# Attention rows: GpSimd adds the attended values to x, and the row's work stands in another order around the transposed maxima

## What is computed

```python
def _L0_xattn_ref(q, k, v):                      # q = x (16,128,256), k = v = ctx_512 (16,128,64)
    QH, KVH = (32, 8)
    D = E // QH                                  # 8
    G = QH // KVH                                # 4
    qh = q.reshape(b, s, KVH, G, D).transpose(0, 2, 3, 1, 4)
    kh = k.reshape(b, s, KVH, D).transpose(0, 2, 1, 3)
    vh = v.reshape(b, s, KVH, D).transpose(0, 2, 1, 3)
    scores = jnp.einsum('bkgsd,bktd->bkgst', qh, kh) * scale
    attn = jax.nn.softmax(scores, axis=-1) / DROPOUT
    out = jnp.einsum('bkgst,bktd->bkgsd', attn, vh)
    return out.transpose(0, 3, 1, 2, 4).reshape(b, s, E)
...
x = _layernorm(x + _L0_xattn_ref(x, ctx_512, ctx_512), axis=-1)
```

## Time and profile before

| | us |
|---|---|
| three runs: median (lowest to highest) | 863.64 (862.07 to 865.16) |
| the profiled execution, its own time | 863.73 |
| its span, first to last instruction | 861.9 |
| TensorE busy, share of the span | 758.5, 88% |
| VectorE busy | 636.6, 74% |
| ScalarE busy | 437.3, 51% |
| GpSimd busy | 345.8, 40% |

### The profile page before, as it was taken

One profiled execution on the slowest core, in us unless ns is written; L12 is line 12 of the kernel. 1 busy time (PEld: TensorE's weight loads), 2 busy tenths in 40 slices (PEclk: granted clock), 3 DMA queues, 4 the chain that ended last, 5 costly groups with the idle time before them and its releaser, 6 DMA issues. The chain is left out here.

```text
span 861.9 us, 18011 instructions
## 1 busy us (share of the span) xinstructions
PE 758.5 (88%) x5790; PEld 403.6 (47%) x5795; DVE 636.6 (74%) x1094; ACT 437.3 (51%) x790; POOL 345.8 (40%) x349
## 2 busy tenths in 40 slices
PE   4699999999999999999999999954689999695773
PEld 1355555555555555555555555533233333243342
DVE  5578677678686687686686887867777778648995
ACT  6444445744455744444754444424367777542333
POOL 5573443754243835333753543316020000105572
PEclk8799999999999999999999999975799999998997
DMA  6721111331211151111112112011140000014411
GB/s 212 309 83 70 76 49 49 113 143 49 96 50 49 50 205 49 49 73 73 49 49 97 49 49 94 4 25 33 24 179 19 19 13 20 6 52 163 179 49 49
DMA packets 23332, 66.13 MB, mean 77 GB/s; under 512 B 7024, under 2 KB 11632, under 8 KB 17648
## 3 DMA queue, kind: packets, MB, share of 16 engines
q1 hardware_dynamic: 23312, 65.90, 20.9%
HBM read 62.55 MB, written 2.42 MB: 75 GB/s over the span
## 5 line engine op out<-in xcount | busy, mean ns | idle before, releaser
L241 POOL TENSOR_TENSOR cum_rows<-cum_rows,cum_t 128x512 f32<-128x512 f32 x128 | 135.8, 1071 | 203.8 <-DMA cum_rows<-cum_scratch 203.8
L560 PE MATMUL pring<-xt_hi,w_hi 128*128 x576 | 172.9, 382 | 6.1 <-DVE gate L485 4.5
L560 PE MATMUL pring<-xt_lo,w_hi 128*128 x576 | 172.3, 381 | 0.0
L560 PE MATMUL pring<-xt_hi,w_lo 128*128 x576 | 171.9, 380 | 0.0
L461 DVE TENSOR_TENSOR bt<-pring,bt 128x512 f16<-128x512 f32 x128 | 88.0, 687 | 73.6 <-ACT bt L333 73.5
L333 ACT CAST bt<-pring 128x512 f16<-128x512 f32 x128 | 74.5, 582 | 129.1 <-PE pring L560 128.9
L465 DVE TENSOR_TENSOR ct<-pring,ct 128x512 f16<-128x512 f32 x128 | 87.9, 687 | 52.9 <-ACT ct L337 52.6
L572 PEld LDWEIGHTS pscore<-ct,bt 128*128 128x128 f16 x1548 | 96.1, 98 | 34.9 <-issue 8.9
L572 PE MATMUL pscore<-ct,bt 128*128 128x128 f16 x1548 | 107.6, 219 | 1.7 <-issue 0.8
L813 DVE TENSOR_REDUCE mx<-bank_at 128x4 f32<-128x512 f32 x128 | 83.1, 677 | 28.3 <-PE bank_at L904 28.0
L337 ACT CAST ct<-pring 128x512 f16<-128x512 f32 x128 | 74.7, 583 | 54.4 <-PE pring L560 54.4
(11 more groups left out here) (153 smaller groups left out, 945.9 us busy)
## 6 DMA issues: line engine op xcount, KB each, us to landing
cum_rows<-cum_scratch SPq DMA_DIRECT2D x32, 1024.0 KB, 4.6
w_raw<-in_w_in SPq DMA_DIRECT2D x36, 256.0 KB, 5.4
weight_b<-weight_scratch SPq DMA_DIRECT2D x8, 1024.0 KB, 6.7
mt<-in_xt SPq DMA_DIRECT2D x4, 512.0 KB, 6.8
acc<-in_x SPq DMA_DIRECT2D x1, 2048.0 KB, 12.0
vals<-in_vals SPq DMA_DIRECT2D x16, 128.0 KB, 2.0
out<-acc SPq DMA_DIRECT2D x4, 512.0 KB, 2.9
w_raw_e<-in_w_up SPq DMA_DIRECT2D x1, 1024.0 KB, 5.0
```

What stands on the lines that cost most here:

```text
L241: nc.gpsimd.tensor_tensor(rows[:, par, q], rows[:, par, q], own, ALU.subtract).then_inc(sem("since"), 1)
L560: mm = nc.tensor.matmul(bank[name][:], w[:, c, k, cols], x[:, k, bass.ds(n % TB, 1), :].rearrange("p o n -> p (o n)"), start=(i == 0), sto ...
```

## The change

It has four parts.

1. `add_heads` moves from VectorE to GpSimd. VectorE's last two adds at the end go too. Where VectorE's own adds ordered its uses of `att`, `divide` now waits until GpSimd has done the add of two divisions earlier (`x_add`); the count starts at one. On GpSimd the adds of rows 0 and 1 stand ahead of the three weight casts, those of rows 2 to 12 in a loop behind them, and the last six between the inverse roots.
2. VectorE's plan: `/0'` goes ahead of M0, and `s1'` stands between M2 and M3, `/1'` between M4 and M5.
3. ScalarE's row: N goes ahead of e1, and `evac_out` of the row before goes behind e2.
4. TensorE's plan: X0 goes from behind F0 D0 to behind F0 D0 F1 F2, D1 D2 follow A1' together, F3 F4 F5 stand together ahead of T1', D3 D4 behind it.

```diff
         @block.gpsimd
         def _(pool):
+            pool.sem_inc(sem("x_add"), 1)
...
+            def add_heads(b, t):
+                pool.wait_ge(sem("att"), 2 * b + t + 2)
+                x = acc[:, bass.ds(b, 1), t * P:t * P + P]
+                nc.gpsimd.tensor_tensor(x, x, att[:, t].unsqueeze(1), ALU.add).then_inc(sem("x_add"), 1)
...
+            for b in range(2):
+                for t in range(2):
+                    add_heads(b, t)
             for i, (name, w) in enumerate((("w_up", w_up), ("w_gate", w_gate), ("w_down", w_down))):
                 pool.wait_ge(sem(f"in_{name}"), 16)
                 nc.gpsimd.tensor_copy(w[:], w_raw[:, i]).then_inc(sem("w_bf16"), 1)
             pool.wait_ge(sem("w_bf16"), 3)
 
+            with pool.Fori(2, BATCH - 3) as b:
+                for t in range(2):
+                    add_heads(b, t)
             pool.wait_ge(sem("in_small"), 16 * 5)
-            for t in range(TB - 1):
-
-                pool.wait_ge(sem("ln_var"), t + 1)
-                r = rstd[:, t * NB:t * NB + NB]
-                nc.gpsimd.tensor_tensor(r, r, expo[:, 0:NB], ALU.pow).then_inc(sem("ln_rstd"), 1)
+            add_heads(BATCH - 3, 0)
+            inverse_root(0)
+            add_heads(BATCH - 3, 1)
+            inverse_root(1)
+            add_heads(BATCH - 2, 0)
+            inverse_root(2)
+            add_heads(BATCH - 2, 1)
+            add_heads(BATCH - 1, 0)
+            add_heads(BATCH - 1, 1)
...
                 exponential(b, 0)
-                exponential(b, 1)
                 if not last:
                     negate_max(b + 1, 1 - slot)
+                exponential(b, 1)
+                exponential(b, 2)
                 if not first:
                     evac_out(b - 1, 1)
-                for i in range(2, 6):
+                for i in range(3, 6):
                     exponential(b, i)
...
             def divide(b, t):
                 dve.wait_ge(sem("rsum"), 2 * b + t + 1)
+                dve.wait_ge(sem("x_add"), 2 * b + t)
...
-            plan = "M0 /0' M1 +0' M2 M3 s1' M4 /1' M5 +1' M6 M7 s0".split()
+            plan = "/0' M0 M1 M2 s1' M3 M4 /1' M5 M6 M7 s0".split()
...
-            plan = "F0 D0 X0 F1 A1' D1 F2 D2 F3 T1' D3 F4 D4 F5 A0 D5 F6 D6 F7 T0 D7".split()
+            plan = "F0 D0 F1 F2 X0 A1' D1 D2 F3 F4 F5 T1' D3 D4 A0 D5 F6 D6 F7 T0 D7".split()
```

More of the change, by code:

```diff
@@ L724, in _, with inverse_root @@
             nc.gpsimd.tensor_tensor(ctx_parts[:, 1, BATCH:], ctx_t[:, BATCH:], ctx_parts[:, 0, BATCH:], ALU.subtract).then_inc(sem("ctx_lo"), 1)
+            def add_heads(b, t):
+                pool.wait_ge(sem("att"), 2 * b + t + 2)
+                x = acc[:, bass.ds(b, 1), t * P:t * P + P]
+                nc.gpsimd.tensor_tensor(x, x, att[:, t].unsqueeze(1), ALU.add).then_inc(sem("x_add"), 1)
+            def inverse_root(t):
+                pool.wait_ge(sem("ln_var"), t + 1)
+                r = rstd[:, t * NB:t * NB + NB]
+                nc.gpsimd.tensor_tensor(r, r, expo[:, 0:NB], ALU.pow).then_inc(sem("ln_rstd"), 1)
+            for b in range(2):
+                for t in range(2):
+                    add_heads(b, t)
             for i, (name, w) in enumerate((("w_up", w_up), ("w_gate", w_gate), ("w_down", w_down))):
@@ L843, in divide @@
                 dve.wait_ge(sem("rsum"), 2 * b + t + 1)
+                dve.wait_ge(sem("x_add"), 2 * b + t)
                 nc.vector.tensor_tensor(att[:, t].rearrange("p (g k d) -> p g k d", k=4, g=4), pturn4[:, :, :, 0:8],
                                         rsum[:, t].unsqueeze(3).broadcast_to([P, 4, 4, 8]), ALU.mult).then_inc(sem("att"), 1)
-            def add_heads(b, t):
-                dve.wait_ge(sem("att"), 2 * b + t + 2)
-                x = acc[:, bass.ds(b, 1), t * P:t * P + P]
-                nc.vector.tensor_tensor(x, x, att[:, t].unsqueeze(1), ALU.add).then_inc(sem("x_add"), 1)
             for i in range(8):
                 row_max(1, 1, i, banks=pmax + ptr[2:4])
-            plan = "M0 /0' M1 +0' M2 M3 s1' M4 /1' M5 +1' M6 M7 s0".split()
+            plan = "/0' M0 M1 M2 s1' M3 M4 /1' M5 M6 M7 s0".split()
             def row(b, slot, first=False, ahead=True):
@@ L868, in row @@
                         if i == 0:
-                            dve.wait_ge(sem("x_add"), 2 * (BATCH - NB))
+                            dve.wait_ge(sem("x_add"), 2 * (BATCH - NB) + 1)
                         if i < 4 * (TB - 1):
@@ L872, in row @@
                     elif what[0] != "M" and not (first and what.endswith("'")):
-                        {"s": invert_sums, "/": divide, "+": add_heads}[what[0]](r, n)
+                        {"s": invert_sums, "/": divide}[what[0]](r, n)
             row(0, 0, first=True)
@@ L882, in _ @@
             divide(BATCH - 1, 0)
-            add_heads(BATCH - 1, 0)
             invert_sums(BATCH - 1, 1)
             divide(BATCH - 1, 1)
-            add_heads(BATCH - 1, 1)
         @block.tensor
```

## The result

| | before | after |
|---|---|---|
| median of the runs shown | 863.05 | 855.35 |
| lowest to highest, runs | 862.07 to 865.16, 4 | 854.02 to 856.25, 4 |
| the profiled execution, its own time | 863.73 | 854.02 |
| its span | 861.9 | 851.9 |

The ratio of the times is 0.9906, with an interval of 0.9882 to 0.993: the changed kernel is faster by 7.7 us, inside the forecast's range and 2.2 us above its figure. The profiled execution of the changed kernel was the fastest of its four (the spans of the others are 852.8 to 854.1), that of before lay 0.7 above its median.

What follows compares the result with a forecast made beforehand. No single engine but a chain through three was taken to set the 7.84 us row. Savings of 7.0 (twelve rows), 2.3 (row 1), 0.6 (row 0) and 0.6 (end) total 10.5 off 863.73: 853.2 us, range 849.8 to 858.5.

Steps and rivals of the forecast that it cites:

- The pace, 0.22 us per matmul, and the chain: Attention rows: matmuls paced at 0.22 us; a chain through three engines sets 7.84 a row, to become 7.20.
- The rival that the change saves nothing: Rows: 0.38 or 0.39 is TensorE's true matmul pace, so only row 1's stall of 1.5 us goes, 862.2; chance 0.07.
- The fork through T0: Behind A0 the new chain splits; ScalarE's copy delays T0, D7 and M7, making X0 come at 7.20.
- The 7.0 us of the sum: Saving claimed for the twelve rows behind row 1: 7.78 each becoming 7.20.
- The row can't fall below 7.0: Floor for an attention row: TensorE's own work without a wait, summed to 7.0 us.
- Row 1: Row 1 goes from 9.48 to 7.20, saving 2.3 us, as VectorE's add no longer waits out a cast.
- Row 0 and the end: Row 0 saves 0.6 us (0 to 1.2); rows 14, 15 and the end save 0.6 (bounds 1.0 and -0.7).
- GpSimd: A 128x128 add moved to GpSimd takes 0.5 us; the Trainium skill's figure gave an estimate of 0.28.
- the cover: GpSimd's casts end near 647; the first division waiting for an add behind them comes near 650, cover 3 us.
- ScalarE tied in: Rows: the new order delays ScalarE's track by 0.35, row 7.55, saving 5.5 us in all, 858.2; chance 0.14.
- The maxima held by an add: GpSimd's add holds VectorE's maxima; 867.1 at an add of 1.07 us, slower from 0.97 on; chance 0.06.
- The clock: TensorE's half clock falls on A1, T1 and the experts' first transposes, end costs 2 us more, 855.5; chance 0.08.

Runs made afterwards that it cites:

- order_only: The three new orders with the adds left on VectorE, against the kernel before: 854.69 us, ratio 0.9893; twelve rows 86.75 us against 93.38.
- again: The changed kernel run and profiled a second time, unchanged: 854.82 us, ratio 0.9905 to the kernel before; end 20.98 us.
- negate_first: The kernel before with only N moved ahead of e1 on ScalarE: 861.32 us, ratio 0.9969; twelve rows 92.46 us, end 19.25.
- held_maxima: The changed kernel plus an idle 128x512 add behind each GpSimd add in rows 2 to 12: 855.82 us, one run; twelve rows 85.50.
- before_unrolled: The kernel before with TensorE's rows 1 to 12 written out instead of looped: 859.75 us, ratio 0.9953; twelve rows 90.11.
- held_adds: order_only plus an idle 128x512 GpSimd add at each division in rows 2 to 12: 865.09 us, one run; twelve rows 90.64.

## Why the prediction was right, and where it was not

**The pace, 0.22 us per matmul, and the chain.** Right up to M5. The chain of before, less the adds, F1 and F5, gives the measured stations of the short row within 0.16: D1 1.28 behind X0 (forecast 1.39), M1 1.70 (1.81), A0 3.47 (3.62), M5 4.89 (5.05). The rival that the change saves nothing, since 0.38 would be the true pace, is out: order_only alone took 6.6 us off the rows.

**The fork through T0.** There, but mis-sized, and not by the forecast's cause. The forecast had T0 5.55 behind X0, D7 6.02, and M7 late by 0.2, with a new wait ahead of it. Measured, T0 comes at 5.34 in the short row and 5.26 in the long one, D7 at 5.78 and 5.69, and M7 waits 0.09 for it. T0 stands 0.21 behind F7, which is TensorE's pace, and 0.15 behind the end of the copy; the last T1 of before followed a copy that it had waited for by 0.05 (749.43 + 0.59 to 750.07), so the copy didn't hold T0. That D7 is late for VectorE is TensorE's own order, not ScalarE's track. And in the loop the row doesn't end over M7, but over M6, D0, F1 and F2, a path that the forecast doesn't name.

**The jump.** Missing. The forecast took TensorE's gaps for the same in every row. D7 to F0 was never looked at on its own, since in the trace of before it lay ahead of a wait. The hint was there, in the row that the forecast was worked out on. In the trace of before F0 comes 0.72 behind D7 at the jump, and 0.32 within the body (652.93 to 653.25):

```profile
645.09 0.38 PE L904 MATMUL bank_at<-k_rows,q_rows 128*128 x1
645.81 0.39 PE L913 MATMUL bank_at<-q_rows,k_rows 128*128 x1 [0.34 <-ACT probs L768]
```

The new order has F0 D0 F1 F2 ahead of X0 where F0 D0 stood, 0.44 more that must fit in before M7 ends, and the jump's 0.4 no longer does. This costs 0.33 in every second row. The two errors have opposite signs: 7.20 was forecast for each row, 7.35 and 7.01 came, a mean of 7.12 over the twelve. The 7.0 us of the sum became 7.9. That the sum of this term was near is luck of the signs, not the mechanism of the forecast.

**"The row can't fall below 7.0".** Wrong: 6.78 with TensorE's rows written out. The floor was added up from gaps in the trace of before (0.15 ahead of each A, A1' at 1.03, T at 0.47), and took them for TensorE's work. In the changed kernel A1' is followed after 1.00 and T0 after 0.44, even in the loop; written out, nearly nothing stands ahead of A1' (0.22 with X0's 0.20 in it) and 0.10 ahead of A0.

**Row 1.** 2.3 forecast, 1.92 came in one trace and 2.07 in the other. The stall of 1.82 is gone, as forecast. No jump lies in this row, so it would be a short one of 7.0, but for a wait of F0 of row 2 for the transfer of N. The row of after shows it:

```profile
636.01 0.39 PE L931 MATMUL bank_at<-q_rows,k_rows 128*128 x1 [0.46 <-DMA q_rows<-neg_mx]
```

**Row 0 and the end.** 0.6 forecast for row 0, 0.80 came, while the stretch ahead of its X0 grew by 0.28 (0.07 in again). 0.6 for the end: 0.45 came in the first trace and -0.88 in the second, against bounds of 1.0 and -0.7, so missed by 0.2 at the low one. T0 follows the last division of batch 14 and no longer the late copy, and A1 follows T0 by 0.55 (forecast 0.5), but both of these 0.4 and 0.5 us were what half the clock had cost before. The forecast saw that for the copy and not for A1: negate_first has the old order and the full clock, T0 0.44 behind the division and A1 0.56 behind T0. Against its 19.25 the new order's end is 0.40 longer. So that 0.45 came for the 0.6 is luck of the clock, not the forecast's mechanism. Half the clock on A1 and T1 costs 1.3 (2 were priced).

**GpSimd.** Forecast 0.5, measured 0.457. From the 4497 ns for 2048 columns of the Trainium skill (GPSIMD Engine Reference, "Elementwise — side-by-side cycle accounting") the forecast had estimated 0.28, in proportion to the columns. The traces agree with its slope: the 512 columns of the idle add take 1271 ns and the 128 columns here 457, so 2.12 ns a column, and its figure is 2.20. What proportion leaves out is a fixed 0.19 us (457 less 128 times 2.12, an estimate from two sizes). The 1071 ns of the earlier trace rows for 512 columns belong to another operation on other operands, and make a worse neighbour. The casts ended at 647.65 (forecast near 647), and the cover held.

**The rivals.** ScalarE tied in: no, T1' and T0 ran without a wait for the copy, and N, ahead of e1, held nobody. The maxima held by an add: no, held_maxima shows it with GpSimd at work nearly four times as long. That rival's turning point was worked out wrong: by its own terms (a row of 7.10 and the add, twelve rows and row 1) the kernel gets slower from an add of 0.81 us on, not 0.97. The clock: real, in some executions; 853.2 and 2 more are 855.2, not 855.5.

**From the trace to the median.** The attention gained 11.1 us in the first trace and 9.9 in the second, and the forecast was 10.5 for it. The medians moved 7.7 and 8.6. Between the first profiled execution (854.02) and the forecast's 853.2 lie 1.2 more ahead of the X0 of row 0, the attention 0.6 shorter, and 0.2 of the rest. Between it and the median lie another 1.3. Both profiled executions of the changed kernel were the fastest of their four, so the gain of 10 to 11 us is that of the favourable cases. That the time lies in the range is shown; that the forecast's 10.5 is what the change is worth in every execution is not. What the others spend their 1 to 3 us on can't be read, since they left no trace. Half the clock in row 0 (2.3 us in before_unrolled, 9.46 against 7.20) or at the end (1.3) has the right size; whether it is that stays open. Why the clock falls in row 0 in some executions wasn't tried either.

## What to carry to other kernels

Close the chain of one round first, then move whatever nobody waits for out of it, into the wait of the engine that is waited on: on top of the rest X0's place gave 3.3 us and the adds 1.3, since a wait could take in one of the two adds anyway, and the jump took in the other in every second row. Before counting on an engine's idle time, look at the gaps between the same two instructions in the middle of a loop's body and at its edge; a jump that a wait hides today is on the path once the wait is gone, and writing the loop out was worth 4 us here after the change. When an elementwise step goes to GpSimd, ask where VectorE's neighbours of it read: reads of PSUM alone weren't held, reads of two SBUF tiles were. And before a gain at the edge of a stretch is claimed, look for a trace of the old order with the full clock there.

## What the hardware showed

- TensorE's jump at the end of a loop's body put 0.4 us more between two matmuls that stand 0.33 apart within it, and 0.22 apart when written out. Where an instruction waits for a count that the loop's counter gives, it came some 0.09 later than written out (0.15 against 0.06 behind the maximum that it waited for, D4 and D0); that the counter's arithmetic is the cause is argued from this, not shown apart.
- An add on VectorE with both inputs in SBUF that overlapped a cast or an add of GpSimd ended 0.14 to 0.15 us behind it, in all cases of before, order_only and held_adds: 281 ns became 858 on average, 1.82 us at most. A maximum from PSUM kept its 688 ns beside casts and adds of GpSimd (66 cases in held_maxima); so did a division of PSUM by SBUF (286 ns), in the few cases that there are.
- An fp32 add of two SBUF tiles on GpSimd over 128 partitions cost 457 ns for 128 columns and 1271 ns for 512.
- The same kernel on the same data had its half clock (1.2 GHz) at 730 to 734 us in one execution, where it cost nothing at the end of the attention, and from 736.5 on in another, where it cost 1.3 us.
